# Routing batches 0 to 3 in pairs, and moving two steps, in the dense stage of a two-layer FFN kernel

## The reference

```
c  = einsum(einsum(x, A[lang]), B[lang]) + emb[lang]            # per batch, rank 16
h  = fq(silu(fq(c) @ fq(w_gate).T) * (fq(c) @ fq(w_up).T))      # fq: rounded to 8 bits and scaled back
x  = x + h @ fq(w_down).T
a  = x + relu(x @ W1[lang] + b1) @ W2[lang] + b2                # per batch
n  = (a - mean(a)) * rsqrt(var(a) + 1e-5) * gamma[lang] + beta[lang]
p  = softmax(n @ Wr);  w, idx = top_k(p, 2);  w = w / sum(w)
x  = x + sum over the two experts of  w * (silu(n @ Wg) * (n @ Wu)) @ Wd
```

## Time and profile before

| | us |
|---|---|
| median of 3 runs | 641.14 (641.02 to 644.41) |
| the profiled execution | 641.35 |
| its span, first to last instruction | 639.7 |

### The profile page before, as it was taken

One profiled execution on the slowest core, in us unless ns is written; L12 is line 12 of the kernel. 1 busy time (PEld: TensorE's weight loads), 2 busy tenths in 40 slices (PEclk: granted clock), 3 DMA queues, 4 the chain that ended last, 5 costly groups with the idle time before them and its releaser, 6 DMA issues.

```text
span 639.7 us, 15484 instructions
## 1 busy us (share of the span) xinstructions
PE 591.5 (92%) x4374; PEld 405.8 (63%) x4374; DVE 497.2 (78%) x1312; ACT 440.9 (69%) x749; POOL 437.0 (68%) x588
## 2 busy tenths in 40 slices
PE   7999889999884779999999999999999999999995
PEld 2243336776662456677777777777777777777773
DVE  5579994888889888898988888888776666666653
ACT  3759996998955648778777878777674555555542
POOL 4106660287875848888887888878888777777654
PEclk9989999999995899999999999999999999999998
DMA  8623001347447449999999999977998888899762
GB/s 268 217 49 93 1 1 51 99 145 223 139 133 248 127 109 195 241 175 196 190 178 187 168 166 190 213 113 111 157 183 121 152 139 141 140 141 140 132 103 34
DMA packets 164066, 92.88 MB, mean 145 GB/s; under 512 B 121476, under 2 KB 156948, under 8 KB 163988
## 3 DMA queue, kind: packets, MB, share of 16 engines
q1 hardware_dynamic: 149284, 72.31, 51.2%
q0 software_dynamic: 14080, 19.54, 20.0%
q10 hardware_dynamic: 624, 0.03, 0.1%
HBM read 44.68 MB, written 18.40 MB: 99 GB/s over the span
## 4 chain that ended last, share of the span: by engine, by line
PE 63%; DVE 16%; DMA 6%; ACT 6%; issue 5%; SPq 2%; POOL 1%; POOLq 0%; DVEq 0%; ACTq 0%
PE ps L709 34%; PE ps L760 17%; PE ps L567 3%; DVE big L1586 2%; DVE small L1219 2%; DMA small<-in_xT 2%; DMA small<-small 1%; PE ps L688 1%; DMA big<-in_Wu 1%; PE ps L585 1%; PE ps L655 1%; DVE big L1432 1%; DVE big L1229 1%; DVE small L1287 1%; DMA big<-in_low 1%
## 5 line engine op out<-in xcount | busy, mean ns | idle before, releaser
L709 PE MATMUL ps<-big,small 128*128 x1608 | 251.7, 313 | 2.3 <-ACT small L998 1.7
L709 PEld LDWEIGHTS ps<-big,small 128*128 128x128 f16 x1608 | 157.0, 98 | 80.8 <-issue 4.4
L1777 POOL DMA_INDIRECT out<-small x67 | 107.6, 1605 | 62.8 <-DVE small L1553 59.2
L760 PE MATMUL ps<-big,small 128*128 x1105 | 131.3, 273 | 1.0 <-DMA small<-small 1.0
L760 PEld LDWEIGHTS ps<-big,small 128*128 128x128 f16 x1105 | 106.4, 98 | 15.1 <-issue 1.2
L1004 ACT ACTIVATE small<-small 128x704 f16<-128x704 f32 x67 | 52.6, 786 | 71.9 <-DVE small L1528 71.5
L1544 DVE SCALAR_TENSOR_TENSOR small<-small 128x64 f16<-128x64 f32 (+1 forms) x134 | 72.6, 583 | 28.5 <-ACT small L1008 28.5
L1745 POOL DMA_INDIRECT small<-rows,small x67 | 79.3, 1184 | 21.0 <-issue 10.6
L1008 ACT ACTIVATE small<-small 128x704 f16<-128x704 f32 x67 | 59.1, 882 | 28.1 <-DVE small L1538 28.1
L1528 DVE SCALAR_TENSOR_TENSOR small<-ps,small 128x704 f32<-128x704 f32 x67 | 63.5, 947 | 18.8 <-PE ps L709 16.9
L1753 POOL TENSOR_SCALAR small<-small 128x1 f32<-128x1 f32 x67 | 71.6, 1069 | 0.0
(11 more groups left out here) (266 smaller groups left out, 1042.0 us busy)
## 6 DMA issues: line engine op xcount, KB each, us to landing
big<-in_Wg SPq DMA_DIRECT2D x8, 704.0 KB, 4.8
big<-in_Wu SPq DMA_DIRECT2D x8, 704.0 KB, 5.8
big<-in_Wd SPq DMA_DIRECT2D x8, 640.0 KB, 5.0
rows<-small SPq DMA_DIRECT2D x8, 518.0 KB, 5.2
big<-in_xT SPq DMA_DIRECT2D x8, 512.0 KB, 6.9
small<-in_xT SPq DMA_DIRECT2D x16, 256.0 KB, 4.6
out<-big SPq DMA_DIRECT2D x16, 256.0 KB, 3.9
small<-small SPq DMA_TRANSPOSE x92, 3.3
```

Source lines behind the costliest of these rows:

```text
L709: m = e.matmul(ps[:, 2 * j + h, 0:352], xsT_(t)[:, 2 * xp + k, :], bigh[:, bass.ds(o + (4 * j + 2 * wp + k) * I + 352 * h, 352)], start=(n ...
L760: m = e.matmul(ps[:, 7, 0:H], hTE_(t)[:, hc_, :], bigh[:, bass.ds(o + 8 * I + (6 * wp + c) * H, H)], start=(n == 0), stop=(n == len(terms) ...
L1777: e.indirect_dma_start(out=out[:, :], out_offset=bass.IndirectOffsetOnAxis(ap=IT[:, t:t + 1], axis=0), in_=yw_(t), in_offset=None, compute ...
```

## The change

`GROUPS` makes the batches 0 and 1, and 2 and 3, one group each; 4 to 7 stay single. `first_choice`, `second_choice`, `second_weight`, `payload` and `slot_hot` take a group: for a pair, one operation works on 8 x 9 values in place of 4 x 9. A pair is chosen in the pass of its second batch, and ranked, placed and paid one pass later. `logits` is two operations per batch in place of four. `payload` writes one weight without a copy, and stands ahead of `variance`. On ScalarE `to_bytes(2b+2)` stands ahead of `squares(2b-1)`. Of the 16 one-hots of the pair 0, 1 GpSimd makes eight one pass later; the second eight of the pair 2, 3 VectorE makes in pass 6, between `payload` and `variance`. Rows of batches 0 and 1, and of 2 and 3, are stored together at i = 8 and i = 12, those of 4 and 5 behind the loop. Some small buffers of the routing move from one SBUF tensor to the other, and `silu` waits for the last `route` since some of them lie where the first tiles' buffers are.

```diff
+        GROUPS = ((0, 1), (2, 3), (4,), (5,), (6,), (7,))
+        ranked_in = {GROUPS[g][-1] + 2: GROUPS[g] for g in range(4)}
...
@@ SP
-                if i % 2 == 0 and i >= 6:
-                    store_rows((i - 6) // 2)
+                if i in (8, 12):
+                    for b in range(i // 2 - 4, i // 2 - 2):
+                        store_rows(b)
+            store_rows(4)
             store_rows(5)
...
@@ TensorE
-                if b < NB:
-                    batch(rank, b - 2)
+                for c in ranked_in.get(b, ()):
+                    rank(c)
...
@@ ScalarE
-            def second_weight(b):
-                w.wait_ge("df", b + 1)
-                w.wait_ge("route", b)
-                e.activation(exd, df, ACT.Exp, scale=xsc[:, 4:5]).then_inc(S["ex"], 1)
+            def second_weight(g):
+                n = 4 * len(GROUPS[g])
+                w.wait_ge("df", g + 1)
+                w.wait_ge("route", g)
+                e.activation(exd[:, 0:n], df[:, 0:n], ACT.Exp, scale=xsc[:, 4:5]).then_inc(S["ex"], 1)
...
             for b in range(-1, NB + 1):
+                step(to_bytes, 2 * b + 2)
                 step(squares, 2 * b - 1)
-                batch(second_weight, b - 2)
-                step(to_bytes, 2 * b + 2)
+                if b in ranked_in or b == NB:
+                    second_weight(group(b - 2))
                 step(relu, 2 * b)
...
@@ VectorE, logits
-                for r in range(2):
-                    for t in range(2):
-                        m = e.scalar_tensor_tensor(Lg[:, 2 * r + t, :], yl[:, r, t, 0:E], rstd[b % 2][:, r, t:t + 1], bWr[:, E * b:E * b + E],
-                                                   ALU.mult, ALU.add)
-                m.then_inc(S["lgt"], 1)
+                e.tensor_tensor(Lb, yl[:, :, :, 0:E].rearrange("p r t n -> p (r t) n"),
+                                rstd[b % 2].rearrange("p r (t a) -> p (r t) a", a=1).to_broadcast([P, 4, E]), ALU.mult).then_inc(S["rt"], 1)
+                w.wait_ge("rt", w.up("rt"))
+                e.tensor_tensor(Lb, Lb, bWr[:, E * b:E * b + E].rearrange("p (a n) -> p a n", a=1).to_broadcast([P, 4, E]), ALU.add).then_inc(S["lgt"], 1)
...
@@ VectorE, payload
-                w.wait_ge("ex", b + 1)
-                e.tensor_scalar(ws, exd, 1.0, None, ALU.add).then_inc(S["rt"], 1)
+                w.wait_ge("ex", g + 1)
+                e.tensor_scalar(ws[:, 0:n], exd[:, 0:n], 1.0, None, ALU.add).then_inc(S["rt"], 1)
...
+            def second_half_of_pair():
+                w.wait_ge("pq", 8)
+                for i in range(8, 16):
+                    m = e.tensor_scalar(lohot[:, 16 + i, :], ioP, slot8[:, i:i + 1], value[:, i:i + 1], ALU.is_equal, ALU.mult)
+                m.then_inc(S["lhv"], 1)
...
@@ VectorE, pass b
-                batch(positions, b - 2)
+                for c in ranked_in.get(b, ()):
+                    positions(c)
+                if b in ranked_in:
+                    payload(group(b - 2))
+                if b == 6:
+                    second_half_of_pair()
                 batch(variance, b - 1)
-                batch(payload, b - 2)
                 step(affine, 2 * b - 4)
                 step(residual, 2 * b + 1)
                 batch(logits, b - 1)
-                batch(first_choice, b - 1)
+                if b - 1 in (1, 3, 4, 5, 6):
+                    first_choice(group(b - 1))
                 if b < 0:
                     widen_h(0)
-                batch(second_choice, b - 1)
+                if b - 1 in (1, 3, 4, 5, 6):
+                    second_choice(group(b - 1))
                 step(gain, 2 * b)
...
@@ GpSimd, pass b
-                batch(slot_hot, b - 2)
+                if b in ranked_in:
+                    slot_hot(group(b - 2))
+                if b == 4:
+                    one_hots(0, range(8, 16))
                 power(b)
```

More of the change, by code:

```diff
@@ L127, in build_program @@
         r16 = carve(small, a, [TILES], F16)
-        pk = [carve(small, a, [8]) for _ in range(2)]
-        near, q128, slot8 = [carve(small, a, [8]) for _ in range(3)]
+        pk = [carve(small, a, [16]) for _ in range(2)]
+        q128, slot8 = [carve(small, a, [16]) for _ in range(2)]
         it5 = [carve(small, a, [SOLO]) for _ in range(4)]
@@ L170, in build_program @@
         pay_at = a[0]
[L171 to L177, removed]
-        OH = carve(small, a, [2, 36], BF16)
+        pay8 = [carve(small, a, [8, PAY]) for _ in range(2)]
+        pay = [pay8[b // 2][:, 4 * (b % 2):4 * (b % 2) + 4, :] for b in range(4)]
+        df = carve(small, a, [8])
+        exd = carve(small, a, [8])
+        m1, k1, m2, k2, ws = [carve(small, a, [8]) for _ in range(5)]
+        OH = carve(small, a, [2, 36], BF16)
+        ar = [8 * 3072 + 3328]
+        Lg, Eq, L2, pos = [carve(big, ar, [8, E]) for _ in range(4)]
+        ohF, poh = [carve(big, ar, [16 * E]) for _ in range(2)]
+        sqj = carve(big, ar, [2, H], BF16)
+        assert ar[0] <= 30464
         cmp9, hot9 = [carve(small, a, [E, E]) for _ in range(2)]
@@ L279, in build_program, with group @@
         EARLY = 2
+        GROUPS = ((0, 1), (2, 3), (4,), (5,), (6,), (7,))
+        def group(b):
+            return b // 2 if b < 4 else b - 2
+        ranked_in = {GROUPS[g][-1] + 2: GROUPS[g] for g in range(4)}
         def use(s, ring):
@@ L355, in psY, with rank_at @@
             return ps[:, 2 + 2 * (s % 2) + t, :]
+        def rank_at(b):
+            return 128 if b % 2 == 0 else 344
         def psC(s, t):
@@ L607, in slots_first @@
                 w.wait_ge("hot", 1)
-                w.wait_ge("lh", 6)
+                w.wait_ge("lh", 4)
+                w.wait_ge("lhv", 1)
                 w.wait_ge("pos", NB - 1)
@@ L1077, in _ @@
             piece_sum(0)
-            second_weight(last)
+            second_weight(5)
             piece_sum(1)
             piece_hi(0)
-            w.wait_ge("ex", NB)
+            w.wait_ge("ex", len(GROUPS))
             e.activation(first_silu[:, 1:2], pcol, ACT.Silu)
@@ L1318, in second_choice @@
                 w.wait_ge("rt", w.up("rt"))
-                w.wait_ge("rk", b - 1)
-                e.tensor_tensor(OH[:, b % 2, :].rearrange("p (t n) -> p t n", t=4), oh1, oh2, ALU.add).then_inc(S["oh"], 1)
-            def payload(b):
-                pv = pay[b % 4]
-                w.wait_ge("ex", b + 1)
-                e.tensor_scalar(ws, exd, 1.0, None, ALU.add).then_inc(S["rt"], 1)
+                w.wait_ge("rk", GROUPS[g][0] if g < 3 else GROUPS[g][0] - 1)
+                o = OH[:, 0:2] if n == 8 else OH[:, GROUPS[g][0] % 2:GROUPS[g][0] % 2 + 1]
@@ new lines, in second_choice, with payload @@
+                e.tensor_tensor(o.rearrange("p a (t n) -> p (a t) n", t=4), chosen(0, n), chosen(1, n), ALU.add).then_inc(S["oh"], 1)
+            def payload(g):
+                b, n = GROUPS[g][0], 4 * len(GROUPS[g])
+                v8 = pay8[(b // 2) % 2][:, 4 * (b % 2):4 * (b % 2) + n, :]
+                pk_ = pk[g % 2][:, 0:2 * n]
+                both_ = slice(0, 2 * n * E)
+                w.wait_ge("ex", g + 1)
+                e.tensor_scalar(ws[:, 0:n], exd[:, 0:n], 1.0, None, ALU.add).then_inc(S["rt"], 1)
@@ L1622, in _ @@
             hot_first()
-            payload(last - 1)
+            payload(4)
             affine(ST - 3)
             logits(last)
-            first_choice(last)
+            first_choice(5)
             token_rows(1, 0, SOLO, it5)
-            second_choice(last)
+            second_choice(5)
             affine(2 * last - 2)
@@ L1631, in _ @@
             positions(last)
-            payload(last)
+            payload(5)
             slot_hot_before_last()
@@ L1820, in _ @@
                 gather(t)
-            slot_hot(last)
+            slot_hot(5)
             side(0)
```

158 lines of the change are left out of this document (88 added, 70 removed).

## The result

The changed kernel took 647.59 us (median of nine runs, 645.57 to 649.99), the kernel before beside it 641.60 (nine runs, 640.71 to 644.41). The ratio is 1.008, 95% interval 1.0062 to 1.0097: slower by 4.0 to 6.2 us. Forecast was 646.0, with 0.58 on slower.

A forecast was written before the change was run, and what follows sets the result against it. No engine was taken as full: the order of waits, through the longer of VectorE's and ScalarE's loops, bounds the dense stage. Last variance 5.27 us later, less 0.43, gives 4.8; 641.14 + 4.8 = 646.0 us, range 641.0 to 648.5.

The forecast's parts named there:

- the seven V: Starts of variance of batches 0 to 6 on VectorE: first forecast 0.97 us later, last 5.27 us later.
- The two loops, and the cast that goes from one wait to the other: Dense-stage period follows the longer loop, VectorE 9.17 or ScalarE 9.66 us; the 1.47 us cast moves idling to second relu.
- Payload ahead of variance: 0: VectorE's payload still needs the exponent issued behind squares, so moving it ahead of variance gains 0 us.
- The late transfer: In b=4, load_xk(9) lands late behind two row stores on SP; VectorE's residual waits 2.8 us.
- The first rival: At load_xk(9) in b=4, the second store delays nothing: 643.2 us, no measurable difference; chance 0.30.
- b=6: 13.04: Period of batch 6: 1.80 with a single payload, 2.07 for eight one-hots on VectorE, 9.17 for its loop: 13.04 us.
- The sum: Whole kernel: last variance start 5.27 us later, less 0.43 behind it, 4.8 us more: 646.0 us.
- Faster, VectorE as the bound: Rival for the dense stage: VectorE alone sets the periods, 59.3 in place of 66.0 us; 634.0 us, chance 0.10.

The follow-up runs named there:

- e7: Kernel before with only ScalarE's cast to bytes moved ahead of squares: 643.07 us, ratio 1.0019 to the kernel before.
- e9: Kernel before with only payload moved ahead of variance, the exponent staying behind squares: 641.24 us, ratio 1.0 to the kernel before.
- e11: Changed kernel with variance ahead of payload and the cast behind squares again, so the pairs alone: 644.33 us, ratio 1.0048 to the kernel before.
- e2: Changed kernel with the cast to bytes put back behind squares and the second gate's exponent: 646.29 us, ratio 1.0058 to the kernel before.
- e3: Changed kernel with ScalarE's exponent of the second gate moved ahead of squares: 645.11 us, ratio 1.0051 to the kernel before.
- e8: Kernel before with the second gate's exponent ahead of squares and payload ahead of variance: 638.61 us, ratio 0.9948 to the kernel before.
- e1: Changed kernel with each pair's second row store issued one pass of SP's loop later: 646.62 us, ratio 1.0065 to the kernel before.
- e4: Changed kernel with VectorE's eight one-hots of b=6 put ahead of payload: 648.53 us, ratio 1.0104 to the kernel before.
- e6: Changed kernel with stores apart, exponent ahead of squares, b=6's one-hots ahead of payload, and the cast back behind squares: 639.85 us, ratio 0.9959 to the kernel before.
- e5: Changed kernel with stores apart, exponent ahead of squares and b=6's one-hots ahead of payload, cast still first: 641.01 us, ratio 0.9984 to the kernel before.

## Why the prediction was right, and where it was off

The mechanisms that it named are in the trace, and most sizes within a few tenths. Less the 1.63 of the later start, the seven V are at 116.02, 125.81, 136.40, 148.00, 161.11, 172.70 and 187.05 (a `payload` start less 0.19 where one stands ahead); forecast were 116.13, 125.98, 136.63, 148.28, 161.74, 173.39 and 186.43.

- *The two loops, and the cast that goes from one wait to the other.* Right. The first four V are within 0.3 us (the fifth, behind the late transfer, is 0.63 early), `relu` idles as foretold (1.3 and more in every period with a payload but the last, 1.19), and e7 shows the cast by itself. In N its price is 1.05 on the kernel before and 3.05 on top of pairs and payload, 1.14 of these from the clock (below); the ratios have it the same, 0.0019 and 0.0022, so that its price depends on the rest is not shown.
- *Payload ahead of variance: 0.* Right in time (e9), and on top of the pairs exactly 0 in N (e11 and e2, both 88.99). The reason given, that payload stays behind the exponent, is shown by e3 and e8: with the exponent moved as well, the same order gains some 2 us on the changed kernel and 3.3 on the kernel before. By itself the order also shortened N by 1.23 in e9, beside shorter operations on VectorE; the prediction had allowed for no gain there, and the time shows none.
- *The late transfer.* Right: 2.43 for 2.8. SP issued the load at 146.94 (forecast 145.07 + 1.63 = 146.70). Mis-sized was the landing: 6.1 us where 5.4 + 1.6 was put. What was taken for the time of the store's bytes is in larger part SP's issue of the load itself, which the prediction left as it was: 1.44 to 1.49 us behind two stores, 0.61 to 0.67 behind one in the kernel before and in e7 to e9. The row of 5.4 was itself a long one: loads right behind one store landed 4.6 to 6.1 after the start of their issue (median 5.0 of 32), right behind two 6.0 to 6.8 (median 6.3 of ten). That leaves some 0.5 of the difference of the medians for the bytes, as an estimate. The first rival, that the store delays nothing, is refuted by e1.
- *b=6: 13.04.* Measured 14.35. The one-hots took 2.14 together and moved the next `residual` by what was forecast (3.72 behind the start of `payload`, forecast 3.87 - 0.19 = 3.68). The 1.31 too little is the term that has `residual` to the next V at 9.17: the `gain` in it waited 1.14 for TensorE, whose clock fell in this execution. Without such a fall, and with the cast and `payload` in their old places, it was 12.82 in e11. That this period is bound by the one-hots alone was wrong: e4 shows the load of x behind them, 0.8 us away.
- *The sum.* -0.69 ahead of b=6 and +1.31 in it, then -0.49 behind the last V for -0.43: 5.40 for 4.8. Two errors partly cancel, and most of the larger is the clock's in this one execution: that the sum comes so near is in part luck.
- *Faster, VectorE as the bound.* Excluded as long as ScalarE's order stands. (Its 10.3 for b=2 is less than the 10.66 worked out above it; with that the rival comes to some 0.4 us more, 634.4 us.) It was the order of two small things, the exponent and the loads of x, that kept the kernel before from running 0.5 to 0.7% faster; the prediction named that wait (0.79 ahead of `variance`) but had no case for what filling it is worth. How much of it the exponent gives by itself, and how much the shorter operations of e9, was not separated.

In N the edits do not add up: cast +1.05, payload -1.23 and pairs +2.35 make +2.17, together they make +5.40. With the clock's 1.14 taken off, 2.1 remains that belongs to no edit alone. The times do not show it: the ratios of e7, e9 and e11 add up to 1.0067, against 1.008 (1.0062 to 1.0097) for the whole change. Whether the edits act on each other, or N varies by as much from one execution to the next, is open. Whether pairs can pay in a good order is open too: e6 has 1.18 more in N than e8, 1.24 more in the median, and their intervals overlap.

## What to carry to other kernels

An operation moved ahead into a wait of its engine gains only if its input is there by then: move its producer with it (e8), or it gains nothing that the time shows (e9). Where two engines wait for each other once per period, as here, filling one wait moves it to the next handover (e7); look for the length of the loop, not for idle time. Batching work that ends in transfers batches the transfers as well: here the load behind them in the queue was issued later, took longer to issue and landed later.

## What the runs showed of the hardware

TensorE's clock fell after short idle times. In the changed kernel TensorE was idle for 2.60 us ahead of `adapter_in` at 179.17; the windows behind it (engine busy times, then granted clock, DMA share and GB/s) show 0.50, the 1.2 GHz level, for some 3.4 us:

```profile
178.00:179.00 1.00, 0.00 (x0) 0.00 (x0) 1.00 (x3) 0.00 (x0) 1.00 (x1) 1.00 0.09 31
...
181.00:182.00 1.00, 1.00 (x7) 1.00 (x6) 0.86 (x6) 1.00 (x3) 1.00 (x2) 0.50 0.15 34
...
184.00:185.00 1.00, 1.00 (x13) 0.90 (x11) 0.96 (x4) 0.85 (x2) 1.00 (x2) 1.00 0.74 222
```

Eight matmuls of the logits took 2.05 us there for 1.11 in the period before, and that is the 1.14 of `gain`'s wait. The idle time ahead of `adapter_in` alone does not decide it: the clock fell to 0.50 behind 2.60 us in the changed kernel, 2.52 in e1 and 2.13 in e5 (shown above), and stayed at 1.00 behind 2.31 in e4, 2.24 in e2, 2.15 in e3 and 2.09 in e11. Of the changed kernel and of e4:

```profile
179.17 1.43 PE L660 MATMUL ps<-big,small 128*128 128x256 f32 x4 [2.60 <-DVE big L1249]
```
```profile
180.07 1.13 PE L660 MATMUL ps<-big,small 128*128 128x256 f32 x4 [2.31 <-DVE big L1249]
```

Where it fell in the same period, `gain` waited for TensorE 1.14 us (the changed kernel) and 1.05 (e1). Each kernel was profiled once, so how often it falls in one kernel is not known.

VectorE's two-input operations on 36 values lengthen from 0.20 to 0.34 us beside GpSimd's one-hots, one here and one there, and one of a pair's choice on 72 values from 0.23 to 0.41 in e2, e3 and e4. Of the changed kernel and of e3, both beside one-hots:

```profile
156.33 0.23 DVE L1339 TENSOR_TENSOR big<-big,small 128x72 f32<-128x72 f32 x1
```
```profile
155.84 0.41 DVE L1339 TENSOR_TENSOR big<-big,small 128x72 f32<-128x72 f32 x1
```

What decides it is not shown. The Trainium skill, page "SBUF — State Buffer", section "Who interferes with whom", has the two engines exclude each other for a whole instruction; the traces agree that they interfere, and no operation of a choice took more than 0.18 us longer, against one-hots of 0.88. The operations of a pair's choice in b=4 on 72 values ran at 0.23 or 0.24 beside GpSimd's one-hots in the changed kernel's trace.
